# Preparing a batch's attention beside the softmax of the batch in front, with one bank of scores

## The reference, cut to what matters

```python
h = _layernorm(x, axis=-1) * (1 + ca) + sa            # norm of the batch, scaled and shifted
q = heads(h @ Wq + bq); k = heads(h @ Wk + bk); v = heads(h @ Wv + bv)
scores = einsum('bhqd,bhkd->bhqk', q, k) * scale * 1.25
threshold = lax.top_k(scores, int(s * 0.2))[0][..., -1:]
scores = scores * jnp.where(scores >= threshold, 1.24, 1.0)
li = conv(scores.mean(axis=-2), conv_w) + conv_b      # one factor per head and key
probs = softmax(scores * li[:, :, None, :])
x = x + ga * (einsum('bhqk,bhkd->bhqd', probs, v) @ Wo + bo)
# the rest: norms, a mixture of 8 experts, a Mamba layer (scan over 256 tokens' states), a second mixture of 8 experts
```

## Time and profile before

| what | value |
|---|---|
| median of three runs | 3508.56 us (3506.55 to 3512.91) |
| the profiled execution | 3520.18 us, its span 3518.9 us |
| busy share PE / DVE / ACT / POOL | 67% / 74% / 44% / 34% |
| granted TensorE clock, mean | 0.80 |

### The profile page before, as it was taken

One profiled execution on the slowest core, in us unless ns is written; L12 is line 12 of the kernel. 1 busy time (PEld: TensorE's weight loads), 2 busy tenths in 40 slices (PEclk: granted clock), 3 DMA queues, 4 the chain that ended last, 5 costly groups with the idle time before them and its releaser, 6 DMA issues.

```text
span 3518.9 us, 34633 instructions
## 1 busy us (share of the span) xinstructions
PE 2374.5 (67%) x8947; PEld 1163.4 (33%) x8947; DVE 2604.5 (74%) x6691; ACT 1565.2 (44%) x3364; POOL 1208.2 (34%) x1118
## 2 busy tenths in 40 slices
PE   3157776867648686777758685486766867586854
PEld 1015221542115431363215531054313632154313
DVE  4864889669886688858896698966998578974182
ACT  2414822665226552547326561165624564263332
POOL 2010336214342143513353142421435134531461
PEclk8578786988769897798869887698878978688957
DMA  3001011041010410132110420104101321113112
GB/s 89 0 18 34 27 40 53 15 117 54 22 44 20 112 54 26 40 94 60 46 50 18 113 60 19 44 17 118 54 26 41 83 60 41 40 31 92 55 48 84
DMA packets 118905, 181.35 MB, mean 52 GB/s; under 512 B 15824, under 2 KB 55392, under 8 KB 115552
## 3 DMA queue, kind: packets, MB, share of 16 engines
q1 hardware_dynamic: 114528, 170.05, 17.4%
q0 software_dynamic: 4096, 8.40, 0.8%
HBM read 156.51 MB, written 21.89 MB: 51 GB/s over the span
## 4 chain that ended last, share of the span: by engine, by line
DVE 33%; PE 28%; issue 12%; ACT 12%; DMA 6%; POOL 4%; DVEq 3%; SPq 2%; another core or an unknown queue 0%; ACTq 0%; POOLq 0%
DVE wmask L679 7%; PE ps_att L930 6%; ACT wmask L661 5%; PE ps_att L941 4%; DVE best L813 4%; DVEq L815 2%; DVE hg L1495 2%; DMA qk<-bounce 2%; PE ps_rest L1435 2%; DMA WG<-in_wgate 2%; DMA bounce<-both_parts 1%; PE ps_att L918 1%; PE ps_rest L1207 1%; DVE wmask L804 1%; PE ps_rest L1666 1%
## 5 line engine op out<-in xcount | busy, mean ns | idle before, releaser
L679 DVE TENSOR_SCALAR_CACHE_REDUCE wmask<-z,tc 128x512 bf16<-128x512 f16 x640 | 432.5, 741 | 23.0 <-ACT z L646 18.9
L1267 POOL TENSOR_TENSOR gat<-sil,cbs 128x512 f32<-128x512 f32 x256 | 324.0, 1268 | 350.9 <-ACT sil L1232 275.3
L1463 ACT ACTIVATE ps_rest<-cols,Aneg 128x512 f32<-128x512 f32 x256 | 176.3, 691 | 522.8 <-DVE hfc L1483 498.9
L847 POOL TENSOR_SCALAR wmask<-wmask 128x512 bf16<-128x512 bf16 x256 | 163.3, 638 | 576.1 <-DVE wmask L804 571.1
L1435 PE MATMUL ps_rest<-hg,ident 128*128 128x512 f32 x256 | 212.9, 927 | 136.3 <-DVE hg L1495 136.2
L1207 PE MATMUL ps_rest<-rest_hT,WF 128*128 128x512 f32 x512 | 281.0, 635 | 27.4 <-ACT sil L1232 27.3
L980 DVE CUSTOM_DVE_ANT_0 z<-ps_att,wmask 128x512 f32<-128x512 f32 x256 | 173.3, 686 | 168.0 <-PE ps_att L918 140.2
L930 PE MATMUL ps_att<-z,Vp 128*32 128x128 f32 x2048 | 282.0, 284 | 7.5 <-DVE both_parts L1002 4.9
L625 PE MATMUL ps_att<-qk 128*128 128x512 bf16 x512 | 231.4, 476 | 81.8 <-DVE g_rank L795 29.8
L758 PE MATMUL ps_att<-wmask,Qpad 128*64 128x512 bf16 x256 | 124.8, 505 | 233.2 <-POOL wmask L847 170.0
L1197 PE MATMUL ps_rest<-gat,WP 128*128 128x512 f32 x512 | 275.5, 623 | 6.3 <-POOL gat L1267 6.1
(11 more groups left out here) (358 smaller groups left out, 5257.4 us busy)
## 6 DMA issues: line engine op xcount, KB each, us to landing
cbs<-spreads SPq DMA_DIRECT2D x128, 256.0 KB, 3.3
WF<-in_w SPq DMA_DIRECT2D x64, 256.0 KB, 2.6
WP<-in_w SPq DMA_DIRECT2D x64, 256.0 KB, 2.6
WF<-in_wfc SPq DMA_DIRECT2D x64, 256.0 KB, 2.7
WG<-in_wgate SPq DMA_DIRECT2D x64, 256.0 KB, 2.9
WP<-in_wproj SPq DMA_DIRECT2D x64, 256.0 KB, 3.4
qk<-bounce SPq DMA_DIRECT2D x32, 384.0 KB, 5.5
bounce<-both_parts SPq DMA_DIRECT2D x72, 128.0 KB
```

The lines of the kernel that those rows point to most:

```text
L679: od.up(dve.tensor_scalar(wmask[:, i, :], z_at[i], tc[:, 0, i:i + 1], None, ALU.is_ge, ALU.add, accum_out=tc[:, 1, i:i + 1]))
L1267: weighed0.up(pool.tensor_tensor(gat[m % 2], sil[m % 2], cbs[e % 2][:], ALU.mult))
```

## The change

The norm, Q, K, V and row factors become threads of their own (`pe_prepares`, `act_prepares`, `dve_prepares`), which belong to the attention's chain. For batches after the first they start once the choice of the batch in front has ended on PE (`masked.all(b - 1)`; on DVE the statistics of the rows wait for `counted.at(b - 1)`), so that they lie beside rescale and softmax of that batch. Everything that they need of PSUM comes from one bank, `att.bank[1]`, used for one thing after the other; each use waits for the reader of the one before. Softmax therefore keeps bank 0 alone for its scores: scores of tile i wait for emph of tile i-1 (before: i-2). V is computed last, after the last product of the batch in front (`mixed.all(b - 1)`), since `Vp` is shared. The context `ctx_` moves out of the K and Q parts into the upper tiles of `z16`, and the projected result into `gsum`. K may only be written once the rescaled K has been cut, and the parts only once they have been sent. The stacked `qk` are loaded after the last scores of the batch in front, as before, by a wait that was there. The constants of `weave` are slightly different.

```diff
+    CTX = 12
+    ctx_ = z16[:, CTX:].rearrange(...)...            # was a view of both_parts
+    def prepare_banks(b):
+        return att.bank if b == 0 else 4 * (att.bank[1],)
     def pe_prepare(b):
+        if b:
+            pe.wait_ge(*masked.all(b - 1))
+        yield from pe_norm(att, b, 0, bk[0])
         k_ps.up(pe.matmul(bk[0][:], wts["Wk"][:], att.hT[:], start=True, stop=True))
+        if b:
+            pe.wait_ge(*kt.at(b))
         q_ps.up(pe.matmul(bk[1][:], wts["Wq"][:], att.hT[:], start=True, stop=True))
...
-        pe.wait_ge(*stacked.at(b, 10))
+        if b:
+            pe.wait_ge(*lens.at(b))
+            yield from pe_turn_q(b)
+            pe.wait_ge(*qread.all(b))
+            pe.wait_ge(*mixed.all(b - 1))
+            yield from pe_values(b)
     def act_prepare(b):
+        if b:
+            act.wait_ge(*splitted.at(b - 1, 2))
         kt.up(act.activation(KT[:], bk[0][:], ACT.Identity, bias=wts["bk"][:]))
+    def dve_rows(b):
+        if b:
+            dve.wait_ge(*counted.at(b - 1))
         yield from dve_norm(att, b, 0, xr[b % 3])
     def dve_prepare(b):
         if b:
-            dve.wait_ge(*proj_ps.at(b - 1))
+            dve.wait_ge(*bounced.at(b - 1, 8))
         dve_split(c1[:], parts, c0[:], splitted)
...
+        yield from dve_guess(b)
+        if b:
+            yield from dve_values(b)
     def pe_refill(b):
+            elif b:
+                free = (projected.at(b - 1), vkept.all(b), attended.at(b - 1))[i]
+                pe.wait_ge(*free)
     def act_refill(b):
+        if b:
+            act.wait_ge(*mixed.all(b - 1))
...
-    lbank, tbank, obank = att.bank[0:2], att.bank[2], att.bank[3]
+    lbank, tbank, obank = att.bank[0], att.bank[2], att.bank[3]
-                if i >= 2:
-                    pe.wait_ge(*emph.at(b, i - 2))
-                scored.up(pe.matmul(lbank[u][:], qs[:, h, j * P:(j + 1) * P], ks[:, h, :], start=True, stop=True))
+                if i:
+                    pe.wait_ge(*emph.at(b, i - 1))
+                scored.up(pe.matmul(lbank[:], qs[:, h, j * P:(j + 1) * P], ks[:, h, :], start=True, stop=True))
...
+    def dve_prepares():
+        for b in every:
+            yield from dve_rows(b)
+            yield from dve_prepare(b)
     def dve_attention():
         for b in every:
-            yield from dve_prepare(b)
-            yield from dve_guess(b)
             yield from dve_search(b)
-    NEAR = 0.1
+    NEAR = 0.05
-           (469.0, 1.1, (("pe", pe_choices()), ...
+           (467.5, 1.12, (("pe", pe_choices()), ...
+                         ("pe", pe_prepares()), ("act", act_prepares()), ("dve", dve_prepares()), ...
```

More of the change, by code:

```diff
@@ L513, in pe_prepare @@
         yield 1.32
[L514 to L519, removed]
+        if b == 0:
+            yield from pe_turn_q(b)
         yield gramd.at(b)
@@ L1029, in dve_project @@
         dve.wait_ge(*outT.at(b))
-        attended.up(dve.tensor_tensor(xr[b % 3][:], xr[b % 3][:], in_tiles(att.bank[1]), ALU.add))
+        attended.up(dve.tensor_tensor(xr[b % 3][:], xr[b % 3][:], in_tiles(tbank), ALU.add))
         yield 0.72
@@ L1089, in pe_mixture0 @@
             pe.wait_ge(*res_rows.all(b - 1))
-        yield from pe_norm(rest, b, 0)
+        yield from pe_norm(rest, b, 0, rest.bank[0])
         yield rest.normed.at(b, 0)
@@ L1094, in pe_mixture0 @@
         yield 1.25
-        yield from pe_norm(rest, b, 1)
+        yield from pe_norm(rest, b, 1, rest.bank[0])
         yield rest.normed.at(b, 1)
@@ L1103, in pe_mixture0 @@
         yield 1.25
-        yield from pe_norm(rest, b, 2)
+        yield from pe_norm(rest, b, 2, rest.bank[0])
         yield rest.normed.at(b, 2)
@@ L1273, in pe_mamba @@
         bk = rest.bank
-        yield from pe_norm(rest, b, 3)
+        yield from pe_norm(rest, b, 3, rest.bank[0])
         yield rest.normed.at(b, 3)
@@ L1311, in act_mamba @@
         c = ((rest.c[0], rest.c[1]), (rest.c[2], cbs[0]))
-        yield from act_norm(rest, b, 3, modT[1][:, b, 1:2], modT[1][:, b, 0:1], rest.hT)
+        yield from act_norm(rest, b, 3, rest.bank[0], modT[1][:, b, 1:2], modT[1][:, b, 0:1], rest.hT)
         for k in range(2 * DC):
@@ L1542, in pe_mixture1 @@
         bk = rest.bank
-        yield from pe_norm(rest, b, 4)
+        yield from pe_norm(rest, b, 4, rest.bank[0])
         yield rest.normed.at(b, 4)
@@ L1568, in act_mixture1 @@
         mod = modT[1][:, b]
-        yield from act_norm(rest, b, 4, mod[:, 4:5], mod[:, 3:4], rest.hT)
+        yield from act_norm(rest, b, 4, rest.bank[0], mod[:, 4:5], mod[:, 3:4], rest.hT)
         yield expl.at(b, 1)
@@ L1814, in emit, with pe_prepares, act_prepares @@
     every = range(B)
+    def pe_prepares():
+        for b in every:
+            yield from pe_prepare(b)
+    def act_prepares():
+        for b in every:
+            yield from act_prepare(b)
+    def dve_prepares():
+        for b in every:
+            yield from dve_rows(b)
+            yield from dve_prepare(b)
     def pe_attention():
         for b in every:
-            yield from pe_prepare(b)
             yield from pe_rescale(b)
```

91 lines of the change are left out of this document (62 added, 29 removed).

## The result

The changed kernel takes 3388.51 us (3381.72 to 3393.52, four runs), against 3509.78 us of the kernel before on the same chip: ratio 0.9653, 95% interval 0.9634 to 0.9673, or 121 us less. Forecast were 3409 us, 100 less. The profiled execution has a span of 3392.3 us, 126.6 under that of before.

The account below looks back on a forecast made before the run. Two unbroken chains slow each other, with idle time in prepare. Removing 332 us, less 116, 32, 42 and 42, saves 100: 3520 to 3420, minus 11.6 to the median, 3409 us; own range 3345 to 3465, 8 in 10 3320 to 3520.

Parts of the forecast that it names:

- What bounds the kernel: Whole kernel: attention and rest are two unbroken chains slowing each other; idle time lies in prepare, 332.4 us in seven stretches.
- the three rivals: One bank decides: 3591 us, chance 0.13; rest does not take it up: 3500 to 3509, 0.09; everything hides: 3293, 0.13.
- The stretches go, the search starts late: Between attentions: seven prepare stretches leave the chain, 332 us; raw scores come 4.5 us late per batch, costing 32 us.
- The step's check: At the search's start: counting DVE instructions of the second experts gave a slow start of about 19 us per batch, against 21.
- The rest's work comes back in search: In search: the rest's 102 us of DVE work from the prepare stretches competes there, costing 116 us.
- PE in softmax and the hand-overs: In softmax: prepare's PE work costs 42 us, and more hand-overs in one queue with stalls of scans another 42 us.
- One bank costs nothing in order: In softmax's scores: emph has 0.7 us to spare before the next scores, so nothing was taken for a tile in order.
- The first and the last stretch keep their length: First attention and last rest: softmax of batch 0 absorbs 8 us of PE work, batch 7's rest runs alone; no change.
- The range: Whole kernel's time: 3345 to 3465 us, from the allowance at 0 and the check to stalls of 14 us per batch.
- the allowance of 42 us: In softmax: 6 us per batch for more hand-overs between engines in one queue and stalls of the scans.

## Why the prediction came out

The time was forecast 20 us too high, and its sign and its main mechanism held. That the number came so near is partly luck: two terms were wrong and cancel, and the sum was made from a trace with the constants of before, at which the change alone is worth 66 us and not 100. By its own steps:

- *What bounds the kernel.* Right. Prepare's stretches were the idle ones, and of the three rivals none came about: scores waited 15.6 us for emph and not over 100; periods shrank by 20.4 us and the last rest started 128.6 us earlier (3088.01 against 3216.56); and not everything was hidden, since rescale, softmax and project grew by 105.8 us. The wait for the experts' weights was read from one batch, 7.79 us; over the six it is 10.6 us each, 63.6 together.
- *The stretches go, the search starts late.* Forecast 332 less 32, measured 311. Raw scores stand 3.1 us behind the addition, not 4.5. The nearness is luck: the step had them 20 us behind the last scores, held by the loads of `qk`; they came 23 to 30 us behind them in six of the seven batches, with no wait for these loads, and the addition itself had moved back. Only behind batch 0 did PE wait for `qk`, 5.2 us. The step's check also set the mean of seven stretches (47.5 us) against a count from six, whose mean is 49.8.
- *The rest's work comes back in search.* Over-sized: 116 forecast, 80 measured. The step assumed that all 102 us of it compete with the search. The order had shown 17 of 40 expert instructions ahead of the addition, where DVE was idle; I used that only for the late start.
- *PE in softmax and the hand-overs.* Under-sized: 84 forecast for both, 105.8 measured, together with the experts' matmuls that moved there: PE is busy 648 us in softmax instead of 566, and by the forecast's own 5.3 us per batch only 37 of these 82 are prepare's. The two errors partly cancel. The choice, which had no term, gave back another 17.6 us, of which DVE's work is 3.9; why the rest of it is denser stays open.
- *One bank costs nothing in order.* Right as far as the runs can tell: 22.6 us of waits and no time lost in the kernel before, with the order that `weave` then finds. The rule of the Trainium skill (Perfetto Trace Analysis, "Optimizing Tensor Performance") that groups should rotate through banks did not bear on this loop, since products and transposes in other banks fill the time between two scores.
- *The first and the last stretch keep their length.* Wrong by 16 us: the last rest starts 41 us behind its attention instead of 33.
- *Not in the sum at all:* the constants, which I had priced at nothing without saying so. The change alone gives 66 us at the old constants and 95 at the new ones (100 against the kernel with prepare put back, ratio 0.9937). The sum of 100 came from rows at the old ones, so like for like it was half too high. The constants add 56 us to the changed kernel and 27 to the one before.
- *The range.* Its lower end, 3345 us, does not come out of what it names: the allowance of 42 us at 0 and the check's 2 us per batch lead from 3409 to 3353.

What stays open: how much of the gain passes through PE's waits for the experts' weights and columns, and what in the loads of `qk` holds the weights up. Both would need the weights' loads ahead of those of `qk`, which was not tried. Open is also how much of each small step is the new order of `weave` and not prepare's place.

The fastest version seen is the changed kernel 1.2 batches ahead: 3390.44 us on a chip where the kernel before takes 3529.14, ratio 0.9609. Its interval does not touch the changed kernel's (0.9634 to 0.9673), though the two ran on different chips.

## What to carry to other kernels

In two interleaved chains look for the stage in which no engine is near its limit, and move that stage beside one that has a limit: here a microsecond of such a stage was worth a third of one over the whole range (0.20 to 0.47 in the single steps), because the other chain's work from it has to go somewhere. Price what is displaced at the idle time of the stage where the order puts it, not at the pace of the busiest one. And where a planner writes the order, its constants and its ties are a change of their own: run the idea with the old and with the new ones before the gain is credited to it, since the two need not add.

## What the runs showed of the hardware

- Loads of 16 KB in place of 256 KB, in the same place of SP's queue, left 55.2 of the 63.6 us that PE waited for them, and the slowest landed 11.7 us after its issue, against 11.3 us. The median fell from 2.9 to 1.8 us. In the batch shown the late ones stood behind 2.1 MB of other loads; in the slowest case size made no difference to how late they landed.
- In five sets of runs, on four chips or more, the kernel before took between 3509.78 and 3536.70 us in the median, 0.8% apart. All comparisons here are ratios to it on the same chip for that reason.
